# A kernel for two conditioned residual layers: x stored by pair, block, part and column, with both parts of a block side by side

## What is computed

```python
# layer 0, on x (8, 256, 1024), mask (8, 1024, 1024) of 0 and 1
out0 = einsum('bsi,oi->bso', x, W0) + b0
diff = einsum('bsi,bio->bso', x, 2 * mask - 1)
x = x + out0 + diff * coeff[:, None, None]
# layer 1, with one of 32 low-rank adapters of rank 16 for each batch
base = einsum('bti,oi->bto', x, W1) + b1
low = einsum('btr,bro->bto', einsum('bti,bir->btr', x, lora_A[slot]), lora_B[slot])
x = x + base + low * 2.0
```

## Time and profile before

| | us |
|---|---|
| median of 3 runs | 379.59 (379.54 to 379.94) |
| profiled execution, its own time | 378.78 |
| its span, first to last instruction | 376.1 |
| TensorE busy in the span | 369.3 |
| DVE busy | 311.2 |
| ACT busy | 205.1 |
| GpSimd busy | 95.9 |

### The profile page before, as it was taken

How to read it: one execution, slowest core, us unless ns; L and a number is a source line. 1 busy time by engine, 2 the same in 40 slices (tenths; PEclk the granted TensorE clock), 3 DMA queues, 4 the chain that set the end, 5 groups by cost and what they waited for, 6 DMA issues and landing times.

```text
span 376.1 us, 5435 instructions
## 1 busy us (share of the span) xinstructions
PE 369.3 (98%) x1934; PEld 311.6 (83%) x1934; DVE 311.2 (83%) x372; ACT 205.1 (55%) x315; POOL 95.9 (25%) x116
## 2 busy tenths in 40 slices
PE   7899999999999999999999999999999999999996
PEld 7789978887888877888788887888878887888875
DVE  4998899999999899986996779964999659977613
ACT  5483765656664767256652567424682466426520
POOL 1355660534007330045001440013300331011300
PEclk9999999999999999999999999999999999999999
DMA  7999999999449694695938869296975959473002
GB/s 252 384 386 335 384 385 360 327 386 319 181 140 288 246 324 178 203 345 187 346 109 289 305 198 361 68 300 247 297 270 142 340 211 320 163 261 124 0 0 112
DMA packets 47691, 94.73 MB, mean 252 GB/s; under 512 B 3610, under 2 KB 4658, under 8 KB 47666
## 3 DMA queue, kind: packets, MB, share of 16 engines
q1 hardware_dynamic: 44848, 85.73, 67.3%
q10 hardware_dynamic: 2754, 8.66, 5.8%
q0 software_dynamic: 64, 0.01, 0.0%
HBM read 86.00 MB, written 8.39 MB: 251 GB/s over the span
## 4 chain that ended last, share of the span: by engine, by line
PE 94%; DMA 2%; SPq 2%; DVE 1%; issue 1%; POOL 0%; ACT 0%; DVEq 0%
PE bank L550 36%; PE bank L519 28%; PE bank L525 14%; PE bank L599 6%; PE bank L561 4%; PE bank L467 2%; PE bank L591 2%; DMA ring_raw<-in_w 2%; PE bank L474 1%; SPq L306 1%; SPq L307 1%; DVE ring_raw L999 1%; DVE ring L1009 0%; SPq L325 0%; POOL ring_raw L389 0%
## 5 line engine op out<-in xcount | busy, mean ns | idle before, releaser
L550 PE MATMUL bank<-w_two,y_two 128*128 128x512 f32 x600 | 141.5, 390 | 0.1
L702 ACT ACTIVATE ring<-ring_raw,coeff_neg 128x1024 fp32r<-128x1024 f32 (+1 forms) x68 | 75.0, 1103 | 110.5 <-DVE ring_raw L999 109.9
L550 PEld LDWEIGHTS bank<-w_two,y_two 128*128 128x128 f32 x600 | 111.6, 188 | 23.9 <-issue 0.3
L519 PE MATMUL bank<-x_two,ring 128*128 128x512 f32 x448 | 126.8, 394 | 0.0
L389 POOL TENSOR_TENSOR ring_raw<-ring_raw,ident 128x128 f32<-128x128 f32 x64 | 50.0, 801 | 217.3 <-DMA ring_raw<-in_w 217.3
L999 DVE SCALAR_TENSOR_TENSOR ring_raw<-ring_raw,coeff_two 128x1024 f32<-128x1024 int32 (+1 forms) x68 | 84.6, 1258 | 13.5 <-DMA ring_raw<-in_mask 11.0
L1009 DVE SCALAR_TENSOR_TENSOR ring<-ring_raw,coeff_neg,ring 128x1024 fp32r<-128x1024 f32 (+1 forms) x68 | 84.2, 1246 | 9.7 <-ACT ring L702 8.9
L519 PEld LDWEIGHTS bank<-x_two,ring 128*128 128x128 f32 x448 | 78.0, 189 | 11.6
L525 PE MATMUL bank<-x_two,ring 128*128 128x256 f32 x448 | 78.0, 281 | 0.0
L525 PEld LDWEIGHTS bank<-x_two,ring 128*128 128x128 f32 x448 | 70.7, 189 | 8.4
L1081 DVE TENSOR_TENSOR y_raw<-bank,y_raw 128x256 f32<-128x256 f32 x56 | 20.6, 417 | 19.3 <-ACT y_raw L740 19.3
(11 more groups left out here) (50 smaller groups left out, 235.4 us busy)
## 6 DMA issues: line engine op xcount, KB each, us to landing
ring_raw<-in_w SPq DMA_DIRECT2D x60, 512.0 KB, 8.4
ring_raw<-in_mask SPq DMA_DIRECT2D x60, 512.0 KB, 9.6
x_both<-in_x SPq DMA_DIRECT2D x31, 256.0 KB, 4.2
out<-z_rows ACTq DMA_DIRECT2D x15, 512.0 KB, 7.7
w_raw<-in_w SPq DMA_DIRECT2D x12, 512.0 KB, 11.4
b_raw<-in_lora_b SPq DMA_DIRECT2D x8, 448.0 KB, 3.6
ring_raw<-in_w SPq DMA_DIRECT2D x8, 256.0 KB, 6.2
ring_raw<-in_mask SPq DMA_DIRECT2D x8, 256.0 KB, 6.4
```

What stands on the lines that cost most here:

```text
L519: pe.matmul(layer0_bank(b, o)[:, 0:2 * T], w, x_two[:, k // PAIR, :, k % PAIR, :], start=(k == 0), stop=False, skip_group_check=True)
L550: ins = pe.matmul(bank[:], y_two[:, q, k, yp, :], w1_two[wp][:, j, k, :], start=(start and k == 0 and n == 0), stop=False, skip_group_chec ...
L702: act.activation(wc_hi[:, e % RING, lo:hi], sums[:, e % RING, lo:hi], ACT.Identity, bias=coeff_neg[:, b:b + 1]).then_inc(wc_hi_done, 1)
```

## The change

It swaps part and block in the layout of x. The order in a partition becomes pair, block, part, column: the two parts of a block are 1 KB each and side by side, 2 KB in one piece, and each part of a pair lies in two pieces of 1 KB, 2 KB apart. All readers and writers follow with their indices. What they do, their number and their order on each engine stay the same, and so does the memory that x takes. The host's layout stays, so a load reads 2 KB in one piece and writes it to two places.

- L519 reads 512 columns in one run, not two runs of 256. L525, L467 and L474 read one run of 256, as before.
- L729 and L1068 work on two runs of 256 in each operand, not on one of 512.
- L325 and L805 write two runs of 256 (1 KB) to each partition, not one of 512 (2 KB).

```diff
--- before.py
+++ after.py
@@ -81,9 +81,9 @@
         wc_hi, wc_lo = ring[:, 0], ring[:, 1]
         w0_at, sums, mask_at = ring_raw[:, 0], ring_raw[:, 1], ring_raw[:, 1].bitcast(I32)
         x_at = ring_at - KT * 2 * T * 4
-        x_both = nc.alloc_sbuf_tensor_at("x_both", [P, XG, 2, PAIR, T], F32, offset=x_at)
-        x_two = nc.alloc_sbuf_tensor_at("x_two", [P, XG, 2, PAIR, T], F32R, offset=x_at)
-        x_raw = x_both[:, :, 1]
+        x_both = nc.alloc_sbuf_tensor_at("x_both", [P, XG, PAIR, 2, T], F32, offset=x_at)
+        x_two = nc.alloc_sbuf_tensor_at("x_two", [P, XG, PAIR, 2, T], F32R, offset=x_at)
+        x_raw = x_both[:, :, :, 1]
         y_at = x_at - 7 * HT * 2 * P * 4
         y_raw = nc.alloc_sbuf_tensor_at("y_raw", [P, 7, HT, 2, P], F32, offset=y_at)
         y_two = nc.alloc_sbuf_tensor_at("y_two", [P, 7, HT, 2, P], F32R, offset=y_at)
@@ -464,14 +464,14 @@
 
                 w = slot(wc_hi, entry(0, u))[:, i, (o % HT) * P:(o % HT + 1) * P]
                 for n in range(2):
-                    pe.matmul(first_bank(o), w, x_two[:, pair(0, u), n, i, :], start=(u % HT == 0 and i == 0 and n == 0), stop=False,
+                    pe.matmul(first_bank(o), w, x_two[:, pair(0, u), i, n, :], start=(u % HT == 0 and i == 0 and n == 0), stop=False,
                               skip_group_check=True)
 
             def first_low(u, i, o):
 
                 last = u % HT == HT - 1 and i == PAIR - 1
                 w = slot(wc_lo, entry(0, u))[:, i, (o % HT) * P:(o % HT + 1) * P]
-                ins = pe.matmul(first_bank(o), w, x_two[:, pair(0, u), 0, i, :], start=False, stop=last, skip_group_check=True)
+                ins = pe.matmul(first_bank(o), w, x_two[:, pair(0, u), i, 0, :], start=False, stop=last, skip_group_check=True)
                 if last:
                     ins.then_inc(y_full, 1)
                 return ins
@@ -516,13 +516,13 @@
                 if k == 0:
                     bank_free(b, o)
                 w = slot(wc_hi, entry(b, u))[:, k % PAIR, (o % HT) * P:(o % HT + 1) * P]
-                pe.matmul(layer0_bank(b, o)[:, 0:2 * T], w, x_two[:, k // PAIR, :, k % PAIR, :], start=(k == 0), stop=False,
+                pe.matmul(layer0_bank(b, o)[:, 0:2 * T], w, x_two[:, k // PAIR, k % PAIR, :, :], start=(k == 0), stop=False,
                           skip_group_check=True)
 
             def unit_low(b, u, k, o):
 
                 w = slot(wc_lo, entry(b, u))[:, k % PAIR, (o % HT) * P:(o % HT + 1) * P]
-                ins = pe.matmul(layer0_bank(b, o)[:, 0:T], w, x_two[:, k // PAIR, 0, k % PAIR, :], start=False, stop=(k == KT - 1),
+                ins = pe.matmul(layer0_bank(b, o)[:, 0:T], w, x_two[:, k // PAIR, k % PAIR, 0, :], start=False, stop=(k == KT - 1),
                                 skip_group_check=True)
                 if k == KT - 1:
                     ins.then_inc(y_full, 1)
@@ -726,7 +726,7 @@
             def x_high(b, g):
                 g = pair(b, g)
                 act.wait_ge(x_in[g], 16 * (b + 1))
-                act.activation(x_two[:, g, 0], x_raw[:, g], ACT.Copy).then_inc(x_hi_done, 1)
+                act.activation(x_two[:, g, :, 0], x_raw[:, g], ACT.Copy).then_inc(x_hi_done, 1)
 
             def y_high_first(o):
 
@@ -1065,7 +1065,7 @@
             def x_low(b, g):
                 dve.wait_ge(x_hi_done, XG * b + g + 1)
                 g = pair(b, g)
-                dve.tensor_tensor(x_two[:, g, 1], x_raw[:, g], x_two[:, g, 0].bitcast(F32), ALU.subtract).then_inc(x_lo_done, 1)
+                dve.tensor_tensor(x_two[:, g, :, 1], x_raw[:, g], x_two[:, g, :, 0].bitcast(F32), ALU.subtract).then_inc(x_lo_done, 1)
 
             def y_low_first(o):
```

## The result

| | before | after |
|---|---|---|
| median of 13 runs, us | 379.86 (378.26 to 381.29) | 381.36 (380.01 to 383.61) |
| profiled execution, its own time | 378.78 | 382.22 |
| its span | 376.1 | 379.5 |

The ratio is 1.0049, with an interval of 1.0034 to 1.0065: the changed kernel is **1.3 to 2.5 us slower**. The forecast was no difference that can be measured, and the range ended at 381.0. One execution of a later experiment (e1_land4) took 742.63 us, twice the usual time; it is in none of the ratios.

A forecast was written before the change was run, and what follows sets the result against it. The prediction took TensorE, busy 98% of 376.1 us, to bound the kernel. Its terms, 0 + 0.01 + 0.3 = +0.3 us, on a previous median of 379.59 gave 379.9 us, with a range from 378.8 to 381.0.

The forecast's parts named there:

- What bounds the kernel: Whole kernel: TensorE, busy 98% of 376.1 us and 94% of the chain of waits; waiting is possible at the start.
- L519's operand, 0: Layer 0's 448 matmuls on TensorE: one run instead of two gains 0, with 2.5 us of gain as the other end.
- The rival of a real seam: L519 on TensorE: the border between two operand runs costs 5.5 ns a matmul, so 377.4 us without it; chance 0.12.
- ACT and DVE, 0.1 us hidden: L729 and L1068: 32 operations each, 3 ns dearer, 0.1 us on each engine, mostly in a gap; 0.01 us counted.
- The pieces, 0.10 us a load: x loads L325 and L805: 256 pieces of 1 KB instead of 128 of 2 KB cost 0.10 us more a load.
- the 0.3 us of the sum: Start of the kernel: three x loads ahead of a w0 block on the chain, 0.10 us each, make +0.3 us.
- The line: DMA price through 88 ns for a 2 KB piece and 164 ns for 4 KB, giving 50 ns for 1 KB.
- "nothing is added" to the issue: SP's issue of x loads: stays at 0.43 us, as L309, already writing two pieces a partition, takes 0.43 too.
- The first x load, late by 0.7 us at most, covered but for 0.1: ACT's first load at the start: smaller pieces in turn-taking queues delay it +0.7 us; +0.1 beyond cover is the bound.
- DVE's cover: DVE at the start: its 0.41 us wait for w0 at 15.05, plus 0.3 of w0 lateness, covers 0.7 us.
- The rival on the slow side: Start: a 1 KB piece costs as much as 2 KB, w0 lands 2.1 us late, 381.7 us, or 384.3; chance 0.16.
- 0.16 for slower: Whole kernel: the chance given to a result slower by over 0.2%, beside 0.72 for the forecast and 0.12 for faster.

The follow-up runs named there:

- e1_land4: Changed kernel, but batch 0's four x loads land in one run of 2 KB a partition in a free area; ratio 0.9997 against the kernel before.
- e5: Kernel before, with layer 0's matmuls in groups of eight L519 and eight L525 for units 0 to 2 of each half; ratio 0.9989.
- e9: Changed kernel, with the host's x stored by block and layer 0's matmuls in groups of eight; ratio 0.9989 against the kernel before.
- e3: Kernel before, but the host stores x by block, so each load reads two runs of 1 KB a partition, 128 KB apart; ratio 0.9997.
- e6: Changed kernel, but the host stores x by block, so loads read two far runs and write two; ratio 1.0005 against the kernel before.
- e10: Changed kernel, with the host's x by block and 1 KB unused behind each 1 KB, source runs 256 KB apart; ratio 1.0005 against the kernel before.
- c0: Kernel before, unchanged, as a run of its own for a second profile; ratio 0.9993.
- e13: Kernel before, with layer 0's matmuls in groups of eight, run a second time; ratio 0.9996.
- e2: Changed kernel, but only the first x load lands in one run of 2 KB a partition in a free area; ratio 1.0003 against the kernel before.
- e11: Changed kernel, with the host's x by block and the first x load issued as two loads; ratio 1.0024 against the kernel before.
- e8: Changed kernel, but the host leaves 256 unused bytes behind each 1 KB of x, source runs 1.25 KB apart; ratio 1.0051 against the kernel before.
- c1: Changed kernel, with no further edit, run once more; ratio 1.0047 against the kernel before.
- e12: Kernel before, but ACT issues the first x load later, behind its activation of h_stack; ratio 1.0066.
- e14: Changed kernel, with 50 transposes ahead of the first real matmul, not 30; ratio 1.0028 against the kernel before.

## Why the prediction was wrong

- **What bounds the kernel** held: TensorE, and waits only at the start.
- **L519's operand, 0**: right. Same 1.07 and 1.09 us, the same 126.8 us for all 448, and e5 and e9 agree to 0.01 us in 1.84. The rival of a real seam is out.
- **ACT and DVE, 0.1 us hidden**: right, and even smaller.
- **The pieces, 0.10 us a load**: neither confirmed nor refuted. The first pair of profiles gives 0.10, the others give 0.02, and the scatter is as large. L599 starts at 22.88 us on average in e3, e6, e9 and e10, and at 22.45 in the four profiles of the old layout (before, c0, e5, e13), near the 0.3 us of the sum; the medians don't show it. With e2 the 31 loads were seen to be hidden, as the text said. The line came from stores of the output at the end of the kernel, not from loads, so "the same kind of transfer" was wrong. The Trainium skill's rule (page "DMA: Bandwidth & Descriptors", the smallest transfer at line rate is 512 B) would have given 0; no run here decides between 0 and 0.10.
- **"nothing is added" to the issue**: wrong. I took L309's 0.43 us for the new shape, but L309's two source runs lie 512 KB apart and x's touch. The issue went from 430 to 610 ns, and SP issued the w0 block of the chain at 7.68 us, not at 7.22. The row was from the wrong kind of load, and one of the right kind stood in the trace of the kernel before: L314 reads 4 KB of W1 in one run and writes it to two places of a partition, and never takes less than 566 ns to issue, where L309 and L325 go down to 367 and 340:

```profile
L314 SPq DMA_DIRECT2D w_raw<-in_w x8: 566/782/1820, 10.6 to 30.6; - x8
```

- **The first x load, late by 0.7 us at most, covered but for 0.1**: this is the step that failed. It is 2.0 us late (8.02 against 6.01), because a load that reads one run and writes two takes 6.8 us to land and not 4.8, of which the prediction had no term. DVE's cover was near what I read: the 2.0 us became 1.47 at L599, so 0.5 was absorbed where I had 0.7. I had bounded the delay from the turns of two queues alone, by the size of a piece, and had no bound for the form of the load. Why the form costs 2.0 us stays open in part (see behind e11). Turn-taking, which the Trainium skill describes on the same page, section "Queues, rings and completion order", is not refuted, but e3, e6, e9 and e10 have the same 1 KB pieces in the same two queues and x_high at 6.04 to 6.71 us, while the kernels with pieces of 2 KB (before, c0, e5, e13) have it at 6.01 to 6.48. So by piece size alone the load is a few tenths of a microsecond late at most, inside the 0.7 of the bound.
- **The rival on the slow side** had the right sign and place and the wrong mechanism. It rested on dear pieces, all loads alike, with the w0 block of 14 us late by 2.1 us; e3, e6 and e10 have the same pieces and no loss, and that w0 block was used by GpSimd at 14.65, 0.6 us later than before, beside a DVE that was late itself. With +2.1 us it came near the measured 1.5 by another way: luck.
- **The chances**: 0.16 for slower was too small for a start where each of three first loads sets the time if it is late.

## What to carry to other kernels

A change of layout in the core's memory is also a change of every load into it: look at both sides of the load, and price its issue and its first landing by a load whose source and destination have the same form, not by one that shares only the piece size. At the start, where no queue has work in stock, one late load is a late kernel; give the first load the plainest form (one run on both sides, or two runs on both sides as in e6), even if the other thirty have another. A sum read from one pair of profiles is not a price before a second profile of the same kernel gives the same sum. A few nanoseconds per matmul that look like the price of an operand's layout should first be looked for where that layout is absent and the neighbours are the same.

## What the runs showed of the hardware

**TensorE's clock can fall behind the gap that a late first x opens.** The granted clock was 1.00 in every stretch of before. e8, where TensorE stands still for 3.4 us after its transposes (stretches of 9 to 12.4, to 15.5 and to 19 us; the clock is the third number from the right):

```profile
9.00:12.40 3.40, 2.09 (x14) 1.89 (x15) 2.82 (x5) 2.28 (x4) 0.00 (x0) 0.94 1.06 386
12.40:15.50 3.10, 3.10 (x16) 3.10 (x16) 3.10 (x5) 1.91 (x3) 0.61 (x2) 0.51 1.06 378
15.50:19.00 3.50, 3.50 (x31) 3.44 (x30) 3.50 (x6) 1.79 (x4) 1.48 (x3) 1.00 1.05 385
```

From 12.4 to 15.5 us it is 0.51, the 1.2 GHz level, and then back at 1.00. The length of the gap does not decide alone: gaps of 2.9 and 3.0 us left the profiled executions of after and c1 at 1.00, while in e12 a gap of 2.3 us was followed by this:

```profile
9.80:12.50 2.70, 2.65 (x13) 2.65 (x14) 2.57 (x4) 1.25 (x2) 0.00 (x0) 0.55 1.05 394
```

The mean clock of an execution was 0.998 or less in 9 of 13 of the changed kernel, in 7 of 12 of c1, 10 of 12 of e8 and 4 of 5 of e12, against 1 of 12 in c0 and 7 of the 159 executions of the kernel before beside the experiments. In the profile of e8 it cost nothing up to L599, which is as late as x (0.8 us behind that of after, both), since DVE's chain sets the pace there.

**The same bytes in the same pieces can be issued and fed at different speeds.** The first x load, as 256 pieces of 1 KB written to two places of each partition, took 460 ns of issue and 5.2 to 5.5 us to land with source runs 128 or 256 KB apart (e6, e10), and 622 to 627 ns and 6.8 to 7.6 us with runs 1 or 1.25 KB apart (after, c1, e14, e8). Whether the distance or the equal steps of the source matter is open.

**A matmul's pitch depends on its neighbours.** 512 columns take 227 ns in a long stretch of their like, 233 in groups of four between 256-column ones, 230 in groups of eight, with one run or two in the operand.
